# Vector quantizer on one core: one index search over up to four score tiles, index rows spread by DMA, score groups of four and three tiles, far one-hots on ScalarE

## The reference, cut to what matters

```python
def stage(res, cb):
    d = jnp.sum(res * res, axis=1, keepdims=True) - 2.0 * jnp.einsum('ne,ke->nk', res, cb) + jnp.sum(cb * cb, axis=1)
    idx = jnp.argmin(d, axis=1)
    q = cb[idx]
    return (res - q, q)
_, qs = jax.lax.scan(stage, x, codebooks)
quant = jnp.sum(qs, axis=0)
```

## Time and profile before

| | us |
|---|---|
| runs of the kernel | 1557.75, 1558.92, 1553.85 (median 1557.75) |
| profiled execution, span from its first to its last instruction | 1554.9 |
| of it: loads and setup, to the first scores | 16.5 |
| periods 0 to 3 | 59.45 |
| periods 4 to 63 | 748.65 |
| drain of the quantizer | 31.1 |
| the three other layers | 699.2 |

### The profile page before, as it was taken

The page is one execution under the profiler, slowest core; times in us unless marked ns, Lnnn a source line. Parts: engine busy times, 40 slices in busy tenths (PEclk is TensorE's granted clock), DMA queues, the critical chain, the costliest instruction groups (busy, mean ns, idle before and its releaser), DMA issues. The chain is left out here.

```text
span 1554.9 us, 34103 instructions
## 1 busy us (share of the span) xinstructions
PE 1363.4 (88%) x11811; PEld 584.3 (38%) x11830; DVE 1247.5 (80%) x5010; ACT 979.4 (63%) x1655; POOL 1045.2 (67%) x772
## 2 busy tenths in 40 slices
PE   5899999999999999999997899995888847777775
PEld 1333333333333333333332566663656611121111
DVE  6999999999999999999998545565222258887886
ACT  2688888888888888888884434431000035766754
POOL 5789999999999999999992133232000029998886
PEclk9999999999999999999999999997999979896977
DMA  8000000000000000000000455321000011202001
GB/s 183 9 1 9 4 9 4 2 9 5 9 4 2 9 4 2 12 2 1 2 2 1 97 122 118 82 46 55 1 2 2 1 49 43 46 1 52 10 14 27
DMA packets 23915, 41.13 MB, mean 26 GB/s; under 512 B 8416, under 2 KB 13792, under 8 KB 23744
## 3 DMA queue, kind: packets, MB, share of 16 engines
q1 hardware_dynamic: 21248, 36.46, 9.9%
q10 hardware_dynamic: 2496, 2.50, 0.7%
HBM read 9.20 MB, written 2.10 MB: 7 GB/s over the span
## 5 line engine op out<-in xcount | busy, mean ns | idle before, releaser
L454 POOL TENSOR_SCALAR l_onehot<-l_ib,c_iota 128x512 bf16<-128x512 f16 x250 | 390.9, 1564 | 47.0 <-ACT l_ib L396 47.0
L567 DVE FIND_INDEX8 l_idx<-l_top,l_scored 128x8 uint32<-128x256 f32 x1024 | 412.9, 419 | 0.0
L247 PE MATMUL ps<-l_ct_slot,l_res 32*128 32x512 f32 x2048 | 406.3, 605 | 0.0
L584 DVE CUSTOM_DVE_ANT_0 l_scored<-ps,l_gain 128x256 f32<-128x256 f32 x1024 | 377.5, 415 | 6.2 <-ACT l_gain L378 5.3
L378 ACT ACTIVATE l_gain<-ps 128x768 f32<-128x768 f32 (+1 forms) x384 | 284.1, 740 | 103.4 <-PE ps L247 99.9
L1812 POOL TENSOR_TENSOR l_isum<-l_term 128x512 f32<-128x512 f32 x160 | 204.9, 1311 | 36.5 <-DVE l_term L1916 21.4
L270 PE MATMUL ps<-l_onehot,l_cbp_slot 128*32 128x512 bf16 x3072 | 213.7, 385 | 4.0 <-ACT l_signed L402 2.6
L241 PE MATMUL ps<-l_csq,l_row_slot 32*128 32x512 bf16 x1024 | 154.2, 393 | 14.6 <-DVE l_top L584 7.4
L1542 PE MATMUL ps<-l_isum,w_l_w_dsc 64*64 64x512 f32 x640 | 106.6, 733 | 61.0 <-POOL l_isum L1812 60.0
L247 PEld LDWEIGHTS ps<-l_ct_slot,l_res 32*128 32x128 f32 x2048 | 155.1, 192 | 10.4 <-issue 0.8
L1732 ACT ACTIVATE ps<-ps,w_l_minus 128x512 f32<-128x512 f32 x192 | 118.5, 662 | 51.2 <-DVE l_term L1922 35.8
(11 more groups left out here) (199 smaller groups left out, 1954.4 us busy)
## 6 DMA issues: line engine op xcount, KB each, us to landing
l_xi<-l_xt SPq DMA_DIRECT2D x120, 128.0 KB
l_xi<-l_xz SPq DMA_DIRECT2D x36, 144.2 KB, 3.1
X<-in_x SPq DMA_DIRECT2D x16, 128.0 KB, 9.1
out<-X SPq DMA_DIRECT2D x16, 128.0 KB, 2.2
l_xr<-l_xt SPq DMA_DIRECT2D x30, 64.0 KB
l_ct<-in_codes_t SPq DMA_DIRECT2D x4, 448.0 KB, 14.7
l_ct_slot<-l_ct SPq DMA_DIRECT2D x7, 256.0 KB, 2.3
l_cbp_slot<-l_cbp SPq DMA_DIRECT2D x8, 96.0 KB, 1.9
```

The lines of the kernel that those rows point to most:

```text
L247: pe.matmul(ps[:, at + n - FIRST[k], :], res[rows, i, P * tt:P * (tt + 1)], ct_slot[rows, par, :], start=False, stop=True, skip_group_chec ...
L454: nc.gpsimd.tensor_scalar(onehot[:, i % 2, g, 0, :], ib16[:, i % 2, g, :], iota[:, 0:1], None, ALU.is_equal).then_inc(s_near, 1)
L567: nc.vector.max_index(idx8[:, i % 2, n, :], top[:, i % 2, n:n + 1].to_broadcast([P, 8]), scored[:, WIDE * (k % 3) + n - FIRST[k], :]).then ...
L584: nc.vector.tensor_tensor_reduce(out=scored[:, WIDE * (k % 3) + m, :], in0=ps[:, WIDE * (k % 2) + m, :PAIRED], in1=gain[:, WIDE * (k % 2) ...
```

## The change

**Groups.** Five groups instead of six, of 4 and 3 tiles in turn and one of 2. Area 0 has four PSUM banks and area 1 three; the bank of the index spread is gone. Even and odd periods have different plans, so that areas go on alternating.

**Search.** `scored` of a group is one row of up to 4 x 256 numbers; tile `m` of a group is multiplied by 4096 to the power `m` (an argument of the same instruction), which, with the scores centred (mean of the codes subtracted) and shifted by a bound, makes the ranges of the tiles disjoint. One search with the group's maxima as its values then finds all indices; the low byte is the pair number. For the shift new small steps stand at the program's start (a maximum over the codes, sums, a square root, the bound, means of the codes), and the means of later stages are taken on ACT (7 operations) and the differences per stage on POOL in periods 1 to 7 (two operations each, in place of one over all stages).

**Indices by DMA.** DVE transposes 128x32 uint16 (`turn`), SP writes that to a scratch tensor in DRAM (128 rows of 64 bytes), waits for it, and reads it back broadcast to all 128 partitions (4 pieces of 1 KB per partition, 512 KB). The 16 matmuls, the cast and the four copies of a period are gone. SP's program is now a loop over the 64 units, with the loads of a stage's codes between.

**One-hots.** All four `near` on POOL at `w - 2`, reading every other byte of `ib`; all four `far` on ACT, two row groups per operation (2 distances and 2 Relus of 128x1024). The middle is added at slot 2 instead of slot 3, the channel sum is at slot 4. In the drain, DVE builds 6 one-hots for each of the last two units.

The core of the diff:

```diff
-GROUPS = (3, 3, 3, 3, 2, 2)
+AREAS = ((0, 4), (4, 3))
+PLANS = (
+    ((0, (0, 4, 8, 12)), (1, (1, 5, 9)), (0, (2, 6, 10, 14)), (1, (7, 11, 15)), (0, (3, 13))),
+    ((1, (4, 8, 12)), (0, (1, 5, 9, 13)), (1, (2, 6, 10)), (0, (3, 7, 11, 15)), (1, (0, 14))),
+)
...
+            for v in range(ALL):
+                par, stage = v % 2, v // UNITS + 1
+                sp.wait_ge(s_turned, START + v + 1)
+                if v >= 2:
+                    sp.wait_ge(s_ib[par], ib_ready(v - 2))
+                sp.dma_start(scratch[par].rearrange("b s c -> (b s) c"), turned[:, par, :]).then_inc(s_wrote[par], 16)
+                sp.wait_ge(s_wrote[par], START + 16 * (v // 2 + 1))
+                if v >= 2:
+                    sp.wait_ge(s_near, START + G * (v - 1))
+                    sp.wait_ge(s_far, far_ready(v - 2))
+                sp.dma_start(ib[:, par],
+                             scratch[par, :, 0:TILES, :].rearrange("b s c -> b (s c)").partition_broadcast(P)
+                             ).then_inc(s_ib[par], 16)
...
-                for tt in range(TT):
-                    n = G * tt + g
-                    mm = pe.matmul(ps[:, SPREAD, P * tt:P * (tt + 1)],
-                                   idx16[:, i % 2, n:n + 1].to_broadcast([P, P]), ident16[:],
...
+                nc.scalar.activation(spread(away[:, g:g + 2, :].rearrange("p g n -> p (g n)")), low(v % 2, g, 2),
+                                     ACT.Abs, bias=minus_iota[:, 1:2]).then_inc(s_away, 1)
...
+                    if k == 0 and fresh is not None:
+                        act.wait_ge(s_ib[fresh % 2], ib_ready(fresh))
...
+                nc.gpsimd.tensor_scalar(spread(onehot[:, v % 2, g, 0, :]), low(v % 2, g, 1), iota[:, 0:1], None,
...
-                for n in range(FIRST[k], END[k]):
-                    nc.vector.max_index(idx8[:, i % 2, n, :], top[:, i % 2, n:n + 1].to_broadcast([P, 8]),
-                                        scored[:, WIDE * (k % 3) + n - FIRST[k], :]).then_inc(s_found, 1)
+                area, tiles = PLANS[w % 2][k]
+                at = (SLOTS * w + k) % 3
+                base, by = tiles[0], tiles[1] - tiles[0]
+                nc.vector.max_index(idx[:, w % 2, base:base + 7 * by + 1:by],
+                                    top[:, w % 2, k, :],
+                                    scored[:, at, 0:len(tiles) * PAIRED]).then_inc(s_found, 1)
...
+                            in0=ps[:, at + m, :PAIRED], in1=gain[:, at + m, :], scale=STEP_UP ** m, scalar=LOWEST,
+                            op0=ALU.add, op1=ALU.max, accum_out=top[:, w % 2, k, m:m + 1]).then_inc(s_top, 1)
+                    if k == 0 and early is not None:
+                        find(early, SLOTS - 1)
+                    if k == 1 and early is not None:
+                        turn(early)
+                    if k == 2 and mid is not None:
+                        add_middle(mid)
```

More of the change, by code:

```diff
@@ L115, in block_l0 @@
         s_first = sem("first_constants")
+        s_clear = sem("clear")
+        s_sums = sem("sums")
+        s_mean = sem("mean")
+        s_all = sem("all_sums")
+        s_roots = sem("roots")
+        s_bound = sem("bound")
         s_square = sem("square")
@@ L155, in block_l0, with back, low, spread @@
         s_border = sem("next_border")
[L157 to L173, removed]
+        def back(w, n):
+            return w - n if 0 <= w - n < ALL else None
+        def low(par, g, n):
+            halves = ib[:, par].bitcast(U8).rearrange("p b (s c two) -> p s b c two", c=C, two=2)
+            return halves[:, TT * g:TT * (g + n), :, :, 0]
+        def spread(tile):
+            return tile.rearrange("p (s b c) -> p s b c", b=TT, c=C)
+        def ib_ready(v):
+            return START + 16 * (v // 2 + 1)
+        def far_ready(v):
+            return START + min(v + 1, POOL_UNITS) * 2 + max(v + 1 - POOL_UNITS, 0)
         block = ctx.enter_context(nc.Block())
@@ new lines, in _ @@
+                    if k == 0 and fresh is not None:
+                        act.wait_ge(s_ib[fresh % 2], ib_ready(fresh))
+                        if fresh >= 2:
+                            act.wait_ge(s_middle, START + fresh - 1)
+                    if fresh is not None:
+                        for what, g in ORDER[k]:
+                            if g or fresh < POOL_UNITS:
+                                if what == "away":
+                                    distance(fresh, g)
+                                else:
+                                    far(fresh, g)
@@ L488, in period @@
                     pool.sem_inc(s_alone, 1)
[L489 removed]
+                    nc.gpsimd.tensor_tensor(product[:, mid % 2, :], res[:, mid % UNITS, :], step[:, mid % KEPT, :],
                                             ALU.mult).then_inc(s_product, 1)
[L491 to L494 removed]
+                for i in KEEPS.get(w, ()):
+                    keep(i)
@@ new lines, in period @@
+                    dve.sem_inc(s_alone, 1)
+                    for m in range(len(tiles)):
+                        nc.vector.tensor_tensor_reduce(
+                            out=scored[:, (SLOTS * w + k) % 3, m * PAIRED:(m + 1) * PAIRED],
+                            in0=ps[:, at + m, :PAIRED], in1=gain[:, at + m, :], scale=STEP_UP ** m, scalar=LOWEST,
+                            op0=ALU.add, op1=ALU.max, accum_out=top[:, w % 2, k, m:m + 1]).then_inc(s_top, 1)
+                    if k == 0 and early is not None:
+                        find(early, SLOTS - 1)
```

584 lines of the change are left out of this document (299 added, 285 removed).

## The result

The changed kernel takes **1498.58 us** (median of 4 runs, 1489.01 to 1499.61); beside it the kernel before took 1558.34 (1553.85 to 1560.05). The ratio is 0.9607, 95% interval 0.9576 to 0.9638: faster by 3.6 to 4.2%. The forecast was 1485.4, the range 1462 to 1530.

What follows compares the result with a forecast made beforehand. DVE and PE were both taken as full at 12.48 us per period. From the profiled 1554.9: -67.8 steady, -7 periods 0 to 3, +1 setup, +1.5 drain = 1482.6; plus 2.85 for the median, 1485.4; range 1462 to 1530.

Steps and rivals of the forecast that it cites:

- The steady period: Periods 4 to 63: 11.35 us each instead of 12.48, saving 67.8 us; a period of 11.2 to 11.6 had chance 0.68.
- Searches: Index searches on DVE: 1.20, 0.93 and 0.66 us for four, three and two tiles, 4.92 per period instead of 6.24.
- DVE above 97%, PE near 89%: Signs in the steady part's profile: DVE busy above 97%, PE near 89% and waiting for `l_top`.
- PE 10.06: PE's steady work per period: five groups at 1.18, four picks at 0.76, channel sum 1.12; worst 11.2 us.
- POOL 10.1 and 1.56 per one-hot: POOL's steady period: four one-hots and three products, 10.1 us; rival that POOL bounds, 12.48 at 2.15 per one-hot, chance 0.06.
- Trip 6.1: Indices through DRAM: 2.2 write, 3.7 read, 0.2 handovers, hidden; rival that it bounds, near 1638 us, chance 0.06.
- the middle costs 0.1 us in its new place: Middle added one group earlier on DVE: a wait of 0.2 us every second period, 0.1 on the mean.
- Drain: End of the quantizer: 1.5 us lost (0 to 4), from the last index trip and ACT's two pairs left.
- Periods 0 to 3: First periods of the quantizer, 59.45 us before: 7 us saved (4 to 9).
- setup: Program start: 1 us lost (0 to 3), from one more DVE pass and tiny steps, beside fewer loads.
- The rival of the clock: PE drops to its lower clock level: a flicker at most, up to 0.5 us per period, 1515 us, chance 0.06.
- The searches' price: DVE rivals: price grows with everything, no gain, about 1557 us, chance 0.04; search cheaper than thought, near 1435, chance 0.05.

Runs made afterwards that it cites:

- e3: Changed kernel with the first matmul of every score tile issued four times, loading TensorE by 3.3 us per period: 1629.4 us, ratio 1.0456.
- e10: Changed kernel with a fifth, unread one-hot of 1.57 us per period on GpSimd: 1516.6 us (single run), period 11.75.
- e11: Changed kernel with the middle added one group later on VectorE (slot 3 again): 1627.4 us (single run), period 13.56.
- e7: Changed kernel with the drain reordered, middle, settling and product ahead of VectorE's six one-hots: 1490.5 us (single run).
- e8: Changed kernel with useless matmuls in TensorE's idle times at the start and in the drain: 1491.9 us (single run).
- e2: Changed kernel with the first matmul of every score tile issued twice, loading TensorE by 1.1 us per period: 1528.1 us, ratio 0.9811.
- e4: Changed kernel with two more waited-for small DRAM writes in the index trip, meant to add 2.9 us: 1534.1 us, ratio 0.9843.
- e1: Changed kernel with each tile searched by itself, every search waiting for the one before: 1683.0 us, ratio 1.0813.
- e5: Changed kernel with each tile searched by itself, without waits inside a group (indices not right): 1565.5 us, ratio 1.0048.
- e12: e11 with six useless matmuls on TensorE ahead of the channel sum: 1550.1 us, ratio 0.9928 to the kernel before.
- e6: Changed kernel with two setup edits, an early square-root table load and codebook maxima taken earlier: 1491.4 us (single run).

## Why the prediction was right

The steady period was forecast at 11.35 and is 11.37, and its parts hold one by one. *Searches*: 1.20, 0.94 and 0.68 against 1.20, 0.93 and 0.66. *Transpose*: 0.14 (421.65 to 421.79) against 0.10. *DVE above 97%, PE near 89%*: 98.7 and 90.1. *PE 10.06*: four tiles cost what three do, 1.18, and e3 gives 10.2. *POOL 10.1 and 1.56 per one-hot*: 1.565, and e10's period fits 10.1 + 1.57. *ACT 1.15 per pair*: 1.14. *Trip 6.1*: 5.35 in the median (the write 1.4 against the 2.2 taken, the read 3.7 as taken). DVE is busy 672.82 / 60 = 11.21 per period and waits 0.15, where the sum had 11.22 and 0.14.

That the middle costs 0.1 us in its new place was right (0.2 on every second period was taken, 0.15 is at 412.57), but e11 shows that the forecast saw only half of that edit: it weighed what the earlier place costs DVE and not what it saves TensorE, 2.15 us per period. The cost of a wait's place was read at one end only.

The forecast was 13 us too low, 12 of them outside the steady periods. In order of size:
- *Drain, mis-sized by 4.8 (1.5 taken, 0 to 4 as bounds, 6.3 measured).* The term counted the trip and ACT's last pairs. It left out that DVE has six one-hots in its queue ahead of the middle (e7), and that TensorE's clock falls after the wait (e8). The earlier trace rows have 0.89 for the clock in the drain of before, against 0.73. By the other traces most of the 4.8 is chance: in e2 the same drain code, after a wait of 5.85 us, had one pair of picks at 2.75 instead of three, and took 28.7 instead of 32.6. With that the stretch would be 33.5, 2.4 above the drain of before and within the bounds. The traced drain of before was of this better kind too, with one pair at 2.75:

```profile
836.41 2.75 PE L270 MATMUL ps<-l_onehot,l_cbp_slot 128*32 128x512 bf16 x24 [0.87 <-ACT l_signed L402]
839.85 1.55 PE L270 MATMUL ps<-l_onehot,l_cbp_slot 128*32 128x512 bf16 x24 [0.69 <-ACT l_step L388]
```

- *Later layers, no term, 4.3.* The code is the same. Over the 13 other executions profiled here these layers took 697.9 to 702.6 us, and 703.5 in this one. It looks like scatter of one execution, and what it comes from was not looked into. The one run of 1489.0, which has no profile, had a mean granted clock of 0.957 against 0.933 to 0.938 in the other three; that it was spared in the drain or in these layers is a guess.
- *Periods 0 to 3, mis-sized by 2.2 (7 taken, 4 as the bound, 4.8 measured).* DVE waits several times for scores at the lower level (clock column 0.68). e8 shows that a higher level in period 0 alone doesn't help; which step of the estimate failed in periods 1 to 3 stays open.
- *Steady part 1.1, setup 0.9*: within their bounds.

Three small sums of the forecast are off, without effect on its result: with 3 x 1.27 for the products, POOL's one-hots pass 12.48 at 2.17 and not 2.15, at 2.0 each the period is 11.8 and not 11.9, and ACT's 10.1 less 0.1 for each of eleven operations is 9.0 and not 9.2 (9.3 was measured, 557.35 / 60).

The rivals: POOL's need is 11.75 - 1.57 = 10.2 by e10, 1.2 us per period below the bound, and the trip of 5.35 is about 2 us below the 7.4 from which e4 shows it to count. The searches' price was as taken. The fixed 2.0 us per DMA that the prediction draws from the Trainium skill (DMA: Bandwidth & Descriptors, Anatomy of one DMA) is stated there for DMAs issued by GpSimd. The trip's are issued by SP, and its small write took 1.4 us in the median. The rival of the clock was set aside because TensorE would be nearly full, and in this order of work the clock column did stay at 1.00, with TensorE busy 90.1%. e11 shows how near it lay: one pass on DVE moved by one group brings a wait of 2.02 us in one piece, and 1.3 us per period through the clock. The Trainium skill (TensorE: Matmul & The Clock Gate, A second HAM failure mode) tells of small idle gaps between groups of matmuls that make the clock swing. In e11 the clock does swing, behind its gaps of 2.02 us. The changed kernel's trace does not agree: from 100 to 700 us it has gaps ahead of half of its score groups, of 1.12 us at most, at a clock column of 1.00.

## What to carry to other kernels

When two engines are full at once, neither half of a change may show anything alone: test it by undoing one half, and don't add a wait while doing so. A mean reserve (1.2 us per period on TensorE) is no reserve at the place where the shortest step of the other engine meets the longest of this one. Before moving an instruction on one engine, ask both who waits for it there and who waits for the buffer it frees; if the matmul engine has to wait in one piece, fill the wait.

## What the hardware showed that was not expected

- A search that waits for the search before it on the same engine comes 0.53 us after it, one that doesn't 0.39: 0.14 us for each such wait (e1, e5).
- Matmuls without use made a kernel 77 us faster (e11, e12). Behind waits of 2.02 us scores of four tiles took 1.93 instead of 1.03 us; behind one of 1.40 the channel sum and the scores after it took their 1.10 and 1.02.
- After the same wait of 5.9 us at the same place, TensorE returned to the higher level after one pair of picks in one execution and after three in others (e2; changed kernel and e6), and the drains are 4 us apart. The length of the wait does not order them: one pair after 8.32 us in e1, three after 6.90 in e5.
- An 8 KB write in 64-byte pieces to DRAM landed in 1.4 us in the median (3.5 at most), less than the 2.2 of the nearest row before.
